# Inputs laid out as used, the first batch of x already turned, and A's products ahead of the first convolutions

## The reference, cut to what matters

```python
# x (64, 64, 1024); conv over the last axis, 9 taps, padding 4, 4 groups of 16 channels
h = conv(x, weight) + (cond @ c_weight.T)[:, :, None] + fside_S_0[None, :, None]
# per block b of 8 samples (gate is (8, 16)):
A_eff = einsum('bn,nri->bri', gate, lora_A)      # (8, 32, 1024)
B_eff = einsum('bn,nor->bor', gate, lora_B)      # (8, 1024, 32)
out = x + h @ kernel + bias + (h @ A_eff[b].T) @ B_eff[b].T + (h @ A_shared.T) @ B_shared.T
```

## Time and profile before

| | us |
|---|---|
| median of 3 runs | 507.1 (506.48 to 507.39) |
| the profiled execution | 507.5 |
| its span, first to last instruction | 505.7 |
| TensorE busy in the span | 488.7 |
| DVE, POOL, ACT busy | 333.0, 272.8, 166.7 |

### The profile page before, as it was taken

The page is one execution under the profiler, slowest core; times in us unless marked ns, Lnnn a source line. Parts: engine busy times, 40 slices in busy tenths (PEclk is TensorE's granted clock), DMA queues, the critical chain, the costliest instruction groups (busy, mean ns, idle before and its releaser), DMA issues.

```text
span 505.7 us, 6792 instructions
## 1 busy us (share of the span) xinstructions
PE 488.7 (97%) x2419; PEld 404.8 (80%) x2419; DVE 333.0 (66%) x385; ACT 166.7 (33%) x210; POOL 272.8 (54%) x157
## 2 busy tenths in 40 slices
PE   2999998999999999999999999999999999999997
PEld 2777787788888888888888888888888888888886
DVE  3887585996939397575938488475947579373502
ACT  1656313341524223331433234331333224241100
POOL 0789952792756529282665619382565718392200
PEclk9999999899999999999999999999999999999999
DMA  8954526852624327241633317241542403252212
GB/s 194 415 211 167 181 61 167 244 211 74 231 104 112 85 53 241 56 123 55 213 119 99 98 31 252 61 119 65 182 150 75 122 12 90 72 121 70 91 35 83
DMA packets 19165, 65.04 MB, mean 129 GB/s; under 512 B 2736, under 2 KB 3632, under 8 KB 18512
## 3 DMA queue, kind: packets, MB, share of 16 engines
q1 hardware_dynamic: 17872, 64.77, 41.6%
q10 hardware_dynamic: 1280, 0.10, 0.2%
HBM read 45.59 MB, written 18.87 MB: 127 GB/s over the span
## 4 chain that ended last, share of the span: by engine, by line
PE 90%; DMA 3%; DVE 2%; POOL 1%; ACT 1%; SPq 1%; issue 0%; ACTq 0%; DVEq 0%
PE main L951 63%; PE rank L964 5%; PE main L956 3%; PE conv L894 3%; PE conv L896 3%; PE conv L895 3%; PE conv L870 2%; DMA cbias<-in_fside_S 2%; PE main L918 1%; PE spare L896 1%; PE spare L895 1%; PE spare L894 1%; PE main L939 1%; SPq L277 1%; DMA b_scratch<-be_lo 1%; PE conv L931 1%
## 5 line engine op out<-in xcount | busy, mean ns | idle before, releaser
L951 PE MATMUL main<-w_hi,y_hi 128*128 128x512 f32 x504 | 157.0, 391 | 0.0
L951 PE MATMUL main<-w_hi,y_lo 128*128 128x512 f32 x504 | 155.9, 389 | 0.0
L951 PE MATMUL main<-w_lo,y_hi 128*128 128x512 f32 x504 | 154.9, 390 | 0.0
L380 POOL TENSOR_TENSOR y_lo<-y_stage,y_hi 128x512 fp32r<-128x512 f32 x56 | 94.1, 1701 | 33.9 <-ACT y_hi L496 33.9
L951 PEld LDWEIGHTS main<-w_lo,y_hi 128*128 128x128 f32 x504 | 94.8, 188 | 20.3
L951 PEld LDWEIGHTS main<-w_hi,y_lo 128*128 128x128 f32 x504 | 94.6, 188 | 20.0
L951 PEld LDWEIGHTS main<-w_hi,y_hi 128*128 128x128 f32 x504 | 93.8, 188 | 19.1
L360 POOL TENSOR_TENSOR xd_lo<-xd,xd_hi 128x512 fp32r<-128x512 f32 x28 | 39.3, 1403 | 104.5 <-ACT xd_hi L507 104.5
L362 POOL TENSOR_TENSOR x_lo<-x_tr,x_hi 128x1024 fp32r<-128x1024 f32 x28 | 82.6, 2949 | 16.4 <-ACT x_hi L509 16.4
L509 ACT ACTIVATE x_hi<-x_tr 128x1024 fp32r<-128x1024 f32 x28 | 57.7, 2060 | 29.8 <-DVE x_tr L655 29.8
L496 ACT ACTIVATE y_hi<-y_stage 128x512 fp32r<-128x512 f32 x56 | 35.5, 633 | 90.4 <-DVE y_stage L673 90.4
(11 more groups left out here) (114 smaller groups left out, 513.4 us busy)
## 6 DMA issues: line engine op xcount, KB each, us to landing
res<-in_x SPq DMA_DIRECT2D x32, 512.0 KB
out<-res SPq DMA_DIRECT2D x31, 512.0 KB
x_in<-in_x_rows SPq DMA_DIRECT2D x7, 2048.0 KB, 12.9
w_raw<-in_L_ffn_kernel SPq DMA_DIRECT2D x4, 1024.0 KB, 17.8
b_cur<-b_scratch SPq DMA_DIRECT2D x21, 128.0 KB, 3.1
la<-in_L_ffn_lora_A SPq DMA_DIRECT2D x4, 512.0 KB, 9.4
lb<-in_L_ffn_lora_B SPq DMA_DIRECT2D x1, 2048.0 KB, 10.3
x_in<-in_x_rows SPq DMA_DIRECT2D x1, 1048.0 KB, 9.0
```

Source lines behind the costliest of these rows:

```text
L380: nc.gpsimd.tensor_tensor(y_parity(y_lo, h, t, e), y_staged(e), y_parity(y_hi, h, t, e).bitcast(F32), ALU.subtract).then_inc(ylo_done, 1)
L951: mm(main[t][:, n * 512:(n + 1) * 512], lhs, rhs[:, k, n * 512:(n + 1) * 512], start=k == 0 and first, stop=False)
```

## The change

All of it is in the prologue and in how the inputs lie in HBM.

1. The gate (each row repeated 8 times), the side bias, the condition and its weights, turned, lie in one array `small` (128 x 140 words), the first transfer on SP's queue. L838, L841, L842 and L970 are gone and so are ACT's L461, L464, L466 and POOL's L332; `cw_rep` is made from `small`. The convolution weights are loaded in rows of 576 bytes and copied into `w_pad` by one more DVE instruction.
2. The first batch of x lies in `x_first` as the transposes leave it, with its zero borders, and goes straight into `x_tr`; its 8 transposes and two memsets are gone.
3. The shared factors lie in `shared`, three times over, in the order in which they are used: one transfer on ACT's queue, one ACT copy for A in place of four, no transpose for B; the low parts are subtracted by DVE, two instructions, in place of five on POOL. They stand ahead of `x_first_low(0)` on DVE.
4. SP's order is: `small`, two loads of A, first piece of x, two loads of A, two quarters of the matrix, second piece of x, bias, two quarters, B. B waits for nothing now.
5. TensorE begins with three products of the identity (256 columns, float32, nobody reads them). `mix_a(0)` and `mix_a(1)` stand ahead of the first convolution, `merge(0)` and `merge(1)` between the first and the second. In `chunk`, the product with the high parts of both comes first for both tiles, then the one with `y_lo`, then the one with `w_lo`, each with a wait of its own.
6. DVE's, ACT's and POOL's orders in the first unit are changed to match.
7. The four stores of `be_hi` wait only for `be_hi`, and those of `be_lo` for `be_lo`. The first `x_high` waits for the four stores of `be_hi` and for `be_lo` being computed, no longer for the stores of `be_lo`.

```diff
         def load_first(eng, half):
-            at, end = ((0, XLOAD), (XLOAD, L))[half]
-            eng.dma_start(x_in[:, :, HALO + at:HALO + end], x_rows[0, :, :, at:end]).then_inc(x_first[half], 16)
+            m0, m1 = ((0, XSPLIT), (XSPLIT, MB))[half]
+            eng.dma_start(x_tr[:, m0:m1, :, :].rearrange("p m n g -> p (m n g)"),
+                          x_first[:, m0 * SB * G:m1 * SB * G]).then_inc(x_first_in[half], 16)
+
+        def load_la(eng, q):
+            eng.dma_start(la[:, q, :], la_v[:, q, :]).then_inc(la_in[q], 16)
 
         def load_w(eng, ma):
             eng.dma_start(w_raw[:, 2 * ma:2 * ma + 2, :].rearrange("p j d -> p (j d)"), kern[ma]).then_inc(kern_in[ma], 16)
...
-        def load_shared(eng, q):
-            eng.dma_start(as_rep[q * R:(q + 1) * R, :], lora_as).then_inc(as_in, 16)
-            eng.dma_start(bs_rep[q * R:(q + 1) * R, :, :], lora_bs.rearrange("(p o) r -> p o r", p=R)).then_inc(bs_in, 16)
...
+            sp.dma_start(sm[:, :], small).then_inc(small_in, 16)
+            for q in range(2):
+                load_la(sp, q)
             load_first(sp, 0)
-            sp.dma_start(gate_nat[:, :], gate).then_inc(gate_in, 16)
-            for q in range(3):
-                load_shared(sp, q)
+            for q in range(2, RQ):
+                load_la(sp, q)
+            load_w(sp, 0)
+            load_w(sp, 1)
+            load_first(sp, 1)
             for oh in range(2):
                 sp.dma_start(bias_nat[oh * 8:(oh + 1) * 8, :], bias_v[oh]).then_inc(bias_in, 16)
-            for q in range(RQ):
-                sp.dma_start(la[:, q, :], la_v[:, q, :]).then_inc(la_in[q], 16)
-            load_w(sp, 0)
-            load_first(sp, 1)
-            for ma in range(1, 4):
-                load_w(sp, ma)
+            load_w(sp, 2)
+            load_w(sp, 3)
+            sp.dma_start(lb[:, :, :].rearrange("p h f -> p (h f)"), lb_v).then_inc(lb_in, 16)
             sp.wait_ge(bias_split, 2)
             for i, t in enumerate((bias_hi, bias_lo)):
                 sp.dma_start(b_cur[STACK + i:STACK + i + 1, :].bitcast(F32), t[:, :].bitcast(F32)).then_inc(bias_put, 16)
-            sp.wait_ge(xt_done, XC)
-            sp.dma_start(lb[:, :, :].rearrange("p h f -> p (h f)"), lb_v).then_inc(lb_in, 16)
...
@@ -268,16 +259,16 @@
                 for q, part in enumerate((be_hi, be_lo, be_hi)):
                     sp.dma_start(b_cur[q * R:(q + 1) * R, oh * 512:(oh + 1) * 512].bitcast(F32),
                                  part[oh * 64:oh * 64 + R, 0, :].bitcast(F32)).then_inc(b_first, 16)
-            sp.wait_ge(be_hid, RQ)
-            sp.wait_ge(be_lod, RQ)
-            for i, part in enumerate((be_hi, be_lo)):
+            for i, (part, split) in enumerate(((be_hi, be_hid), (be_lo, be_lod))):
+                sp.wait_ge(split, RQ)
                 for oh in range(2):
                     for bq in range(2):
                         row = oh * 64 + bq * R
                         sp.dma_start(b_scratch[i, bq * 4:(bq + 1) * 4, :, oh * 512:(oh + 1) * 512].rearrange("b r d -> r b d"),
-                                     part[row:row + R, :, :].bitcast(F32)).then_inc(be_out, 16)
+                                     part[row:row + R, :, :].bitcast(F32)).then_inc(be_out[i], 16)
             sp.wait_ge(b_first, 96)
-            sp.wait_ge(be_out, 128)
+            sp.wait_ge(be_out[0], 64)
+            sp.wait_ge(be_out[1], 64)
...
             y_low_first(0)
+            w_low(0)
             y_low_first(1)
-            w_low(0)
             w_low(1)
             w_low(2)
+            pool.wait_ge(bias_split, 1)
+            nc.gpsimd.tensor_tensor(bias_lo[:, :], bias_nat[:, :], bias_hi[:, :].bitcast(F32),
+                                    ALU.subtract).then_inc(bias_split, 1)
...
+            act.dma_start(w_nat[:, :], conv_w.rearrange("o c k -> o (c k)")).then_inc(cw_in, 16)
+            act.dma_start(sh_in[0:STACK, :, :].rearrange("p f d -> p (f d)"), shared).then_inc(shared_in, 16)
+            act.wait_ge(small_in, 16)
+            nc.scalar.activation(cw_rep[:, :, :, :], small_part(3).rearrange("p (g c) -> p g c", g=G)
...
+
+            act.wait_ge(shared_in, 16)
+            nc.scalar.activation(as_st[0:STACK, :, :].rearrange("p k m -> p (k m)"), sh_in[0:STACK, 0, :], ACT.Copy).then_inc(as_hi, 1)
+            nc.scalar.activation(bs_st[0:STACK, :], sh_in[0:STACK, 1, :], ACT.Copy).then_inc(bs_hi, 1)
 
             def x_first_high(half):
-                act.wait_ge(xt_done, (half + 1) * XH)
+                act.wait_ge(x_first_in[half], 16)
+                if half:
+                    act.wait_ge(halo_zero, 1)
                 for t in range(2):
                     nc.scalar.activation(x_part(x_hi[:, t], half), x_raw(t, *x_half(half)), ACT.Copy).then_inc(x0_hi, 1)
...
-                                     ACT.Copy).then_inc(as_hi, 1)
-            act.wait_ge(bs_turned, 1)
-            nc.scalar.activation(bs_st[0:STACK, :], bs_t[0:STACK, :], ACT.Copy).then_inc(bs_hi, 1)
...
@@ -500,7 +465,8 @@
                 if isinstance(u, int) and u == 2:
                     act.wait_ge(conv_ready, 2 * CT)
                     act.wait_ge(b_first, 96)
-                    act.wait_ge(be_out, 128)
+                    act.wait_ge(be_out[0], 64)
+                    act.wait_ge(be_lod, RQ)
...
             y_high_first(0, 0, FIRST)
+            w_high(0)
             y_high_first(0, 1, FIRST)
-            w_high(0)
             w_high(1)
             w_high(2)
             x_first_high(1)
+            act.wait_ge(bias_in, 32)
+            nc.scalar.activation(bias_hi[:, :], bias_nat[:, :], ACT.Copy).then_inc(bias_split, 1)
             w_high(3)
...
+
+            dve.wait_ge(diag_done, 1)
+            dve.wait_ge(small_in, 16)
+            nc.vector.tensor_tensor(gmix[:, :, :], diag[:, :].unsqueeze(1).broadcast_to([P, NB, R8]),
+                                    small_part(0).unsqueeze(2).broadcast_to([P, NB, R8]), ALU.mult).then_inc(gmix_done, 1)
             t_low(0)
             t_low(1)
+            dve.wait_ge(ctx_mm, 1)
+            nc.vector.tensor_tensor(ctx_all[:, :, :], rank[:, 256:512].rearrange("p (g n) -> p g n", g=G),
+                                    small_part(1).unsqueeze(2).broadcast_to([P, G, NS]), ALU.add).then_inc(ctx_done, 1)
+
+            dve.wait_ge(as_hi, 1)
+            as_part = as_st[2 * R:STACK, :, :].rearrange("p k m -> p (k m)")
+            nc.vector.tensor_tensor(as_part, sh_in[2 * R:STACK, 0, :], as_part.bitcast(F32), ALU.subtract).then_inc(as_lo, 1)
+            dve.wait_ge(bs_hi, 1)
+            nc.vector.tensor_tensor(bs_st[R:2 * R, :], sh_in[R:2 * R, 1, :], bs_st[R:2 * R, :].bitcast(F32),
+                                    ALU.subtract).then_inc(bs_lo, 1)
             x_first_low(0)
-            dve.wait_ge(ctx_mm, 1)
-            dve.wait_ge(cond_cp, 2)
-            nc.vector.tensor_tensor(ctx_all[:, :, :], rank[:, 256:512].rearrange("p (g n) -> p g n", g=G),
-                                    cb_col[:, :].unsqueeze(2).broadcast_to([P, G, NS]), ALU.add).then_inc(ctx_done, 1)
-            dve.wait_ge(bs_in, 48)
-            nc.vector.transpose(bs_t[0:STACK, :].rearrange("r (p o) -> r o p", p=R), bs_rep[0:STACK, :, :]).then_inc(bs_turned, 1)
-            dve.wait_ge(diag_done, 1)
-            dve.wait_ge(gate_tr, 1)
-            nc.vector.tensor_tensor(gmix[:, :, :], diag[:, :].unsqueeze(1).broadcast_to([P, NB, R8]),
-                                    spare[:, 0:NB].unsqueeze(2).broadcast_to([P, NB, R8]), ALU.mult).then_inc(gmix_done, 1)
+            a_turn(0)
             dve.wait_ge(ctx_done, 1)
             y_tile(0, 0, 0, FIRST, first=True)
+            a_turn(1)
             y_tile(0, 0, 1, FIRST, first=True)
-            a_turn(0)
+            w_add(0)
+            w_add(1)
+            a_turn(2)
             dve.wait_ge(t01_copied, 1)
             nc.vector.tensor_tensor(t01_raw[:, :, :, :].rearrange("p g s c -> p s g c"),
                                     main[0][:, 0:512].rearrange("p (s g c) -> p s g c", s=J, g=G),
                                     t01_raw[:, :, :, :].rearrange("p g s c -> p s g c"), ALU.add).then_inc(t01_sum, 1)
-            a_turn(1)
-            w_add(0)
-            w_add(1)
-            a_turn(2)
             w_add(2)
             w_add(3)
             a_turn(3)
-            dve.wait_ge(x_first[1], 16)
-            for c in range(XH, XH + 2):
-                x_turn(0, c)
-            w_add(4)
-            w_add(5)
-            for c in range(XH + 2, XC):
-                x_turn(0, c)
-            w_add(6)
-            w_add(7)
+            for m in range(4, 8):
+                w_add(m)
             x_first_low(1)
             y_tile(0, 0, 2, FIRST, first=True)
             w_add(8)
@@ -824,7 +785,10 @@
         def _(pe):
             mm = nc.tensor.matmul
 
+
             pe.wait_ge(ident_ready, 2)
+            for _ in range(3):
```

(65 more changed lines are left out.)

107 lines of the change are left out of this document (25 added, 82 removed).

## The result

| | before | after |
|---|---|---|
| median, us | 507.25 (506.48 to 508.42, 4 runs) | 498.96 (498.63 to 500.07, 4 runs) |
| profiled execution, us | 507.5 | 500.07 |
| its span, us | 505.7 | 498.2 |

The ratio is 0.9843, interval 0.9819 to 0.9866. The medians differ by 8.3 us, the two profiled spans by 7.5: the profiled execution after is the slowest of its four.

A forecast was written before the change was run, and what follows sets the result against it. TensorE, busy 488.7 of 505.7 us, was taken as the bound, with only idle time and half-rate products to gain. 5.0 (start) + 3.8 (stores) = 8.8 us gave 498.3 us; likeliest range 496.5 to 500.5, eight in ten 495.0 to 502.3.

The forecast's parts named there:

- The stores: Before the second batch's fast convolution: splitting B's stores removes TensorE's idle 2.75 us, gaining 3.8 us, bounds 0 and 4.5.
- The half rate behind the stall: After TensorE's 2.75 us wait before 89.59: 1.2 in place of 2.4 GHz over 3.6 us, costing 1.8 us more.
- The start: Prologue up to the end of slice 1: TensorE gets through it earlier, gaining 5.0 us, bounds 2.5 and 8.
- The running sum of bytes: First loads: 0.22 MB by 4.0 us, then 412 GB/s; a transfer lands 1.8 us after its bytes are through.
- the half rate: First convolution's tail and the second convolution: TensorE at 1.2 GHz after gaps costs up to 1.5 us; 0.5 taken.
- The wait inside `chunk(0)`: In the first unit: TensorE wants the second `y_lo` at 25.5, POOL has it at 26.1, costing 0.6 us.
- A: Loads at the start come at the old rate: chain 2.5 to 3 us later, gain 2.2 + 3.8, 501.1 us; chance 0.2.
- B: TensorE leads: DVE's chain is shorter and TensorE waits for nothing, 8 + 4.5 gained, 494.6 us; chance 0.12.
- C: Before the second batch, DVE's second difference or POOL late by 1 us or more: 501.1 to 502 us; chance 0.1.
- D: Slower: TensorE at 1.2 GHz from 9.0 us through slice 1, 8.9 later less 3.8, 512.2 us; chance 0.03.
- E: In the loop: a later wait absorbs the shift, so nothing that counts changes, 507 us; chance 0.02.

The follow-up runs named there:

- The two later measurements: The changed kernel measured twice more with no edit: 499.20 us (0.9857) and 499.21 us (0.9845).
- the two runs on it: Changed kernel with B's stores waiting together again: 503.79 us (0.9955); kernel before with only B's stores split: 503.46 us (0.9947).

## Why the prediction was right

**Sum.** 8.8 us forecast, 8.3 by the medians and 7.5 by the profiled spans; 498.3 against 498.96. The two later measurements gave 7.4 and 7.8. The mechanism was right in both parts; that the median came within 0.7 us is partly luck. The profiled execution was 1.4 above its forecast (500.07 against 498.7), but it also lay 1.1 above the median, where I had allowed 0.4.

**The stores.** 3.8 forecast; 7.52 - 3.52 = 4.0 in the profile, 4.0 also in the two other profiles of the changed kernel, 3.0 and 4.6 by the medians of the two runs on it. The next late thing was DVE's difference, as said: it ended at 77.74, TensorE's first fast convolution did not wait, and the second tile waited 0.29 us, where 0.7 was given back in the sum. The half rate behind the stall was worth 1.5 and not 1.8: from the one fast convolution to the next it was 8.35 us before (89.59 to 97.94), and is 6.81 now without the wait. With 2.75 and less 0.29 that makes the 4.0. The chain was right step for step: every duration in it was in the trace.

**The start** was the term that was too large: 5.0 forecast, 3.5 in the profile (4.4 and 3.9 in the two later ones). Step by step: the transposes began at 4.52 (5.1 forecast; the weights were there at 2.98, at my lower bound of 3), the side term ended in time, the shared low parts took 1.22 each (1.2). Then the landings: `shared` came at 10.6 (8 to 9), the second load of A at 10.9 (9.9), x at 13.4 (12.6). The running sum of bytes was good to 1 us for the one queue and 1.6 to 2.6 off for `shared` on a queue of its own, which I had let run ahead; what it had to spare before x took that up. The second miss is the half rate: the first convolution's end and the second (17.41 to 19.86, 2.45 in place of 1.5), then `y_tile(1)` at 19.97 in place of 18.1. I had charged 0.5 for it. In this profile it was near 1.0, an estimate: `merge(2)` came 1.26 later than in the first of the two later profiles (22.50 against 21.24), of which x explains 0.28 (13.42 against 13.14). In those two profiles it lay elsewhere or was absent. 0.8 for x and 1.0 for the clock make up the 1.9 by which `chunk(0)` began late (25.98 against 24.1). The profile without half rate there says the same: x 1.5 late (14.06), `chunk(0)` 1.6 late (25.66). The wait inside `chunk(0)` was 0.40, forecast 0.6. One sum of mine was 0.2 off: slices 0 and 1 with their merges took 5.98 us before (29.75 to 35.73), so that 24.1 with the 0.6 leads to 30.7, not 30.5.

**The rivals.** A (data at the old rate): no, x landed at 13.4, not at 15.5; but it lay nearer than B. B (TensorE leads): no, it waited for A's load, x, DVE and POOL, once each. C (the stall in another form): 0.29 us was left. D (slower through the clock): half rate over 3.5 of 16 us, no more; but the runs with x ahead and with the old order show the direction, with 4.6 and 5.8 us idle and every product of the next convolution at half rate. Its price was too high in any case: I doubled all of the 11.7 us, and the four mixes in it, 7.5 us, take as long at half rate (1.95 and 2.07 us measured there). E: no.

**What I did not see** is how much the order of TensorE and the order of DVE hang together (5.9 us lost with TensorE's undone, 2.3 with both undone). The prediction had both as given.

## What to carry to other kernels

Where one transfer must be waited for, fill the wait with work whose data is smaller and comes first, and move the consumers on the other engines in the same step; with TensorE's order undone alone 5.9 us were lost here, with both undone 2.3. A semaphore that guards a buffer should wait for the last reader of that buffer, not for the last of a group of transfers: here one condition was worth 4.0 us of idle time and clock in the profiles, 3.0 and 4.6 by the medians. When data is moved up in a queue, ask which transfer is now late, and which engine takes that one first.
